# A mask added in the tiling of the attention scores, and the scores computed in two sets

## The chip, the cores and the metric

The kernel runs on one core of a Trainium2 chip. The metric is the device time of one execution in microseconds (us). TensorE multiplies matrices into PSUM banks, VectorE and ScalarE read PSUM and work on rows, GpSimd (POOL) works on SBUF and issues indirect transfers, SyncE issues most of the other transfers.

## The reference, cut to what matters

Two transformer layers over 64 sequences of 64 tokens of width 128. Each has a layer norm, a cross attention to a context of 64 tokens per sequence with 16 heads of width 8, and a mixture of experts (one of 8 experts in layer 0, two of 16 in layer 1). Only the attention of layer 0 has a mask:

```
x = x + tanh(g_xattn[0]) * attention0(layernorm(x), ctx, ctx, mask)   # 16 heads
    scores = where(mask == 0, -1e9, q @ k.T);  softmax(scores / sqrt(8)) @ v
x = x + tanh(g_ffn[0]) * top1_of_8_experts(layernorm(x))
x = x + tanh(g_xattn[1]) * attention1(layernorm(x), ctx, ctx)         # no mask
x = x + tanh(g_ffn[1]) * top2_of_16_experts(layernorm(x))
```

## The kernel before

The 4096 tokens are 32 tiles of 128 rows, two sequences each. Tiles are taken in ten groups of 2, 2, 4, 4, 4, 4, 4, 4, 2, 2 (SIZES), for layer 0 and again for layer 1, so tiles count from 0 to 63; a unit is a pair of tiles. The stages of the trace are: attention of layer 0 (with its router) to about 170 us, experts of layer 0 to about 275 us, attention of layer 1 to about 425 us, then the experts of layer 1.

The order of the work on each engine is written out by hand. A step has a list of items (tiles, units or groups) and a function that gives each item a place in time, counted in tiles; run() sorts all steps of an engine by that place and, within one place, by their order in the list. `shift(-2)` for tile t is place t - 2, `head(-4)` for a group is its first tile - 4, `tail(3)` its last tile + 3. Each engine works off its list in order; waits on semaphores (`wait_ge`) keep the engines together.

For one tile t the attention goes like this:

- GpSimd builds k_blk (L427): the keys of four heads side by side with zeros elsewhere, in a ring of two.
- TensorE computes scores (L852): for each of two sequences b and four row groups q of 32 rows (four heads each) one f32 product of 32 x 64 weights and 256 columns, at the position (32 q, 64 b) of the array. Row groups 0 and 1 go into S_ps[0], 2 and 3 into S_ps[1], each two PSUM banks. It waits for qT, for k_blk, and for `shifted` to show that both halves of tile t - 1 were read.
- In layer 0 the mask goes into the banks ahead of the scores (L829): an identity of 128 x 128 in bf16 times mask_bias (0 or -2^100), a bank at a time, over four heads. mask_first does S_ps[0], at the place t - 2 behind the transposes of the tile before, as soon as its first half was subtracted; score does S_ps[1] and then all products, at the place t - 1.
- VectorE takes for each half h the maximum over keys (L593) and subtracts it (L601), which frees that half of the banks: maximum(0), subtract(0), maximum(1), subtract(1), at the place t - 1. Both halves wait for the one semaphore `scored`.
- TensorE transposes each half (L863; half 0 at the place t - 1, half 1 at the place t), ScalarE takes exp (L530), TensorE multiplies with the values (L878), VectorE divides (L609, L612).

Around this, per group or unit, run the projections of q, k and v (L825, L737, L748), the output (L895) and its addition on VectorE (L620), and the router's turns, logits and ranks. TensorE's list within one place is: score, turn_probs(1), ranks, attend, logits, turn_av, project_q, output, project_v, project_k, turn_probs(0), mask_first, turn_r, turn_x.

The raw mask is loaded by SyncE per group (L401) as 128 rows x 64 columns of int32 per tile, eleven tiles ahead, in a ring of four, and cast by VectorE per group four tiles ahead (L648). SyncE's list holds x, ctxT, the mask, and the rows kept for the second layer (L406).

Of the kernel before, what the change touches and what calls it, by code (L numbers as in the profile page):

```python
# [6 lines left out]
BF16 = mybir.dt.bfloat16  # L7
# [7 lines left out]
H, DK = 16, 8  # L15
# [108 lines left out]
def head(skew):  # L124
    return lambda g: g.first + skew


def tail(skew):
    return lambda g: g.last + skew
# [55 lines left out]
def attention(nc, ctx, space, x_all, r_xn, ws, dram, rs, hooks):  # L185
# [67 lines left out]
    ctx_loaded = [sem(f"ctx_loaded{k}") for k in range(CR)]  # L253
    mask_loaded = [sem(f"mask_loaded{k}") for k in range(R)]
    kept = [sem("kept_full"), sem("kept_rest")]
# [16 lines left out]
    kblk_ready = sem("kblk_ready")  # L272
    scored = sem("scored")
    max_ready = sem("max_ready")
    shifted = sem("shifted")
# [38 lines left out]
    def of(layer):  # L314
# [26 lines left out]
        def dram_rows(g):  # L341
            return slice(g.local * P, (g.local + g.n) * P)
# [41 lines left out]
        def sync_steps(sp):  # L384
            def load_x(g):
                if g.i >= 4:
                    sp.wait_ge(ln_stats, units_to(g.i - 4))
                from_ = dram["x"] if masked else r["x_mid"]
                sp.dma_start(x_group(g), from_[dram_rows(g), :].rearrange("(u p) d -> p u d", p=P)).then_inc(x_in[g.at(4)], 16)

            def load_ctx(g):
                if g.i >= CR:
                    sp.wait_ge(k_made, g.i - CR + 1)
                    sp.wait_ge(v_made, units_to(g.i - CR))
                sp.dma_start(ctxT[:, g.at(CR), 0:g.n, :],
                             dram["ctxT"][:, dram_rows(g)].rearrange("d (u p) -> d u p", p=P)).then_inc(ctx_loaded[g.at(CR)], 16)

            def load_mask(g):
                if g.i >= R:
                    sp.wait_ge(mask_made, g.i - R + 1)  # L400
                sp.dma_start(mask_in[:, g.at(R), 0:g.n, :],  # L401
                             dram["mask"][dram_rows(g), :].rearrange("(u p) k -> p u k", p=P)).then_inc(mask_loaded[g.at(R)], 16)
# [186 lines left out]
        def vector(dve):  # L589
            def maximum(h):  # L590
                def step(t):
                    dve.wait_ge(scored, t + 1)
                    nc.vector.tensor_reduce(maxes[:, t % 2, h, :, :], half_of(h), X, ALU.max).then_inc(max_ready, 1)  # L593
                return step
# [48 lines left out]

            def mask(g):
                n, at = g.n, g.at(R)
                dve.wait_ge(mask_loaded[at], 16 * (g.i // R + 1))
                wait(dve, scored, tiles_to(g.i - R))
                nc.vector.tensor_scalar(mask_bias[:, at, 0:n, :], mask_in[:, at, 0:n, :], 0.0, MASKED, ALU.is_equal, ALU.mult).then_inc(mask_made, 1)  # L648

# [71 lines left out]
            if masked:  # L721
                steps += [(choose, groups, settled(6, 11, short, later)), (rows, groups, settled(7, 12, short, later)), (mask, groups, head(-4))]
# [44 lines left out]
        def tensor(pe):  # L767
# [58 lines left out]

            def mask_half(h, g, u):
                for k in range(2):
                    nc.tensor.matmul(S_ps[h][:, k, 0:HQ * S].rearrange("p (e k) -> p e k", k=S), w["ident_bf"][:, :],  # L829
                                     mask_bias[:, g.at(R), u, :].unsqueeze(1).to_broadcast([P, HQ, S]),  # L830
                                     start=True, stop=False, skip_group_check=True)

            def mask_first(t):
                g = GROUP_OF[t]
                pe.wait_ge(mask_made, g.i + 1)
                if t == 0:
                    pe.wait_ge(r["casts"], 1)
                wait(pe, shifted, 2 * t - 1)
                mask_half(0, g, t - g.first)

            def score(t):
                g = GROUP_OF[t]
                u = t - g.first
                pe.wait_ge(qT_ready, g.i + 1)
                pe.wait_ge(kblk_ready, t + 1)
                wait(pe, shifted, 2 * t)
                if masked:
                    mask_half(1, g, u)
                for b in range(2):
                    for q in range(4):  # L850
# [4 lines left out]
                last.then_inc(scored, 1)  # L855

# [43 lines left out]
            awake += [] if masked else [(lambda n: stream_into(T_ps, n), [Q], lambda _: NT - 1)]  # L900
            steps = [score_ahead] + awake + [(turn_probs(1), tiles, shift(0)),
                     (rank if masked else rank_slots, groups, settled(7 if masked else 8, 12, short, later)), (attend, tiles, shift(1)), (logit, groups[:7], settled(6, 9, short, later)),
                     (turn_av, groups, tail(2)), (project_q, groups, head(-2)), (output, groups, tail(3)),
                     (logit, groups[7:], settled(6, 9, short, later)),
                     (project_v, late_units, unit_head(-1)), (project_k, late, head(-3)),
                     (turn_probs(0), tiles, shift(-1)), (mask_first, tiles if masked else [], shift(-2)), (turn_r, groups, settled(5, 8, short, later)), (turn_x, groups, turn_x_at)]
            run(hook["first_tensor"](pe) + steps + hook["tensor"](pe))
# [628 lines left out]

IN_A = [("ident", P), ("wq", D), ("wk", D), ("bq", 1), ("bk", 1), ("bv", 1), ("head_rows", H // 4), ("tile_at", 1), ("row_at", 1)]
IN_B = [("wv", D), ("wo", D), ("before0", P), ("before1", P), ("ones1", P), ("router0", E0), ("router1", E1)]
# [33 lines left out]
def program(nc, d, out):  # L1572
    with ExitStack() as ctx:
# [18 lines left out]
        w1.update(cut(col_1, IN_1))  # L1592
        w0.update(bo=w0["bo0"], minus_half=sb("minus_half", [P, Q]), eps=sb("eps", [P, Q]), ident_bf=sb("ident_bf", [P, P], BF16))
        w1.update(bo=w0["bo1"])
# [16 lines left out]
        r1.update(before=bf["before1_bf"], ones=bf["ones1_bf"], router=w0["router1"])  # L1611
        r0["pads"] = Space(nc, space.at).take("pads", [P, PADS, RW])
        f1 = r1["f1"] = {"in": sem("f1_weights_in")}
        for name, shape in (("gate", [P, E1, HID1]), ("fc", [P, E1, HID1]), ("proj", [P, E1 // 2, D])):
            f1[name] = sb("f1_" + name, shape)
        for name, shape, dt in (("logits", [P, NT, E1], F32), ("top", [P, NT, 8], F32), ("top_at", [P, NT, 8], U32), ("slot", [P, 2, NT], F32),
                                ("sent", [P, 2, NT], F32), ("gap", [P, NT], F32), ("total", [P, NT], F32)):
            r1[name] = sb("r1_" + name, shape, dt)

        late = Space(nc, space.at)  # L1620
# [41 lines left out]
        def lay_bv(_):  # L1662
            vec = nc.vector
            vec.wait_ge(in_a, 16)
            vec.tensor_copy(bv_rows[:, 0, :], w0["bv"].to_broadcast([P, P])).then_inc(bv_laid, 1)
            vec.tensor_copy(w0["ident_bf"][:, :], w0["ident"][:, :]).then_inc(r0["casts"], 1)
            vec.wait_ge(in_1, 16)
            vec.tensor_copy(bv_rows[:, 1, :], w1["bv"].to_broadcast([P, P])).then_inc(bv_laid, 1)
# [207 lines left out]
```

## Time and profile before

| | |
|---|---|
| time before, median of 3 runs | 513.66 us (513.63 to 516.26) |
| the profiled execution | 512.48 us, its span 510.7 us |
| granted TensorE clock, mean | 0.983 |
| busy share of the span | PE 86 %, DVE 70 %, ACT 63 %, POOL 53 % |
| chain that ended last, by engine | PE 43 %, DVE 23 %, issue 18 %, POOL 7 % |
| data moved in the first 12.8 us | 209 GB/s |

A busy PE is not PE at its peak, since the ends of matmuls are modelled. PE is TensorE, DVE VectorE, ACT ScalarE. A line such as L852 is that of the kernel before.

### The profile page before, as it was taken

The numbers are of one execution on the slowest core, as the hardware profiler recorded it, in microseconds if no ns is written. First come the engines' busy times: TensorE is split into PE (matmuls) and PEld (weight loads), VectorE is DVE, ScalarE is ACT, GpSimd is POOL, SyncE is SP. The second block draws the span as 40 slices with busy tenths as digits, with TensorE's granted clock in tenths as the row PEclk, the third lists the DMA queues.
The fourth block names the chain that finished last, engine by engine and source line by source line (L and its number), as shares of the span: only waits on it lengthen the run. The fifth ranks groups of instructions, "written<-read, shape, count | busy, mean of one in ns | idle before, by whom it ended". The sixth has DMA issues, their size and how long they took to land.

```text
span 510.7 us, 21982 instructions
## 1 busy us (share of the span) xinstructions
PE 438.4 (86%) x8481; PEld 321.1 (63%) x8481; DVE 359.5 (70%) x949; ACT 322.7 (63%) x755; POOL 272.7 (53%) x325
## 2 busy tenths in 40 slices
PE   2788999799978785999998789998999688798986
PEld 1455677567756685999983456666667456554544
DVE  5778879878778765455541788889998787664555
ACT  2555575566766783677754556776778467676663
POOL 2632535545475268888886544544552481544444
PEclk9999999999999998899999899999999899999999
DMA  7225434232110145565436001110031000000112
GB/s 209 51 57 153 98 104 126 70 106 71 46 55 29 35 126 101 78 97 71 45 35 148 14 4 45 46 33 3 25 85 35 23 4 4 3 1 16 43 42 68
DMA packets 50629, 30.69 MB, mean 60 GB/s; under 512 B 12384, under 2 KB 46944, under 8 KB 50528
## 3 DMA queue, kind: packets, MB, share of 16 engines
q1 hardware_dynamic: 37072, 18.54, 13.6%
q0 software_dynamic: 6640, 4.67, 7.0%
q10 hardware_dynamic: 6816, 6.07, 4.2%
q8 instruction: 70, 1.15, 0.9%
q14 instruction: 31, 0.25, 0.2%
HBM read 19.41 MB, written 9.85 MB: 57 GB/s over the span
## 4 chain that ended last, share of the span: by engine, by line
PE 43%; DVE 23%; issue 18%; POOL 7%; ACT 4%; DMA 3%; ACTq 1%; DVEq 1%; POOLq 0%; SPq 0%
DVE maxes L593 8%; PE S_ps L852 6%; PE T_ps L863 5%; POOL x_mid L1145 4%; PE A_ps L878 4%; PE m_H_ps L1478 3%; DVE prob L601 3%; PE S_ps L829 2%; PE m_X_ps L1505 2%; PE Q_ps L825 2%; PE m_T_ps L1518 2%; PE f_H_ps L1197 2%; PE Q_ps L737 2%; PE m_X_ps L1489 2%; PE m_X_ps L1461 2%
## 5 line engine op out<-in xcount | busy, mean ns | idle before, releaser
L593 DVE TENSOR_REDUCE maxes<-S_ps 128x8 f32<-128x512 f32 x128 | 87.6, 685 | 40.5 <-PE S_ps L852 40.5
L427 POOL TENSOR_TENSOR k_blk<-kT,col_a 128x512 f32<-128x512 f32 x64 | 67.7, 1068 | 77.7 <-ACT kT L488 54.5
L530 ACT ACTIVATE probT<-T_ps 128x512 f32<-128x512 f32 x128 | 76.0, 594 | 43.5 <-PE T_ps L863 42.8
L863 PE MATMUL T_ps<-col_a,prob 128*128 128x128 f32 x512 | 83.4, 287 | 9.8 <-DVE prob L601 6.1
L601 DVE TENSOR_TENSOR prob<-S_ps,maxes 128x512 f32<-128x512 f32 x128 | 88.5, 692 | 4.4
L863 PEld LDWEIGHTS T_ps<-col_a,prob 128*128 128x128 f32 x512 | 56.7, 143 | 48.0 <-issue 34.4
L1145 POOL DMA_INDIRECT x_mid<-f_out,f_rows x39 | 60.9, 1562 | 11.9 <-issue 11.9
L852 PE MATMUL S_ps<-k_blk,qT 32*64 32x256 f32 x1024 | 46.5, 415 | 5.0 <-DVE prob L601 4.1
L1010 DVE TENSOR_TENSOR f_hid<-f_H_ps,f_b 128x512 f32<-128x512 f32 x39 | 27.0, 692 | 32.4 <-PE f_Y_ps L1211 27.0
L878 PE MATMUL A_ps<-v_blk,probT 128*32 128x18 f32 x4096 | 48.7, 187 | 0.2 <-issue 0.2
L878 PEld LDWEIGHTS A_ps<-v_blk,probT 128*32 128x32 f32 x4096 | 42.0, 110 | 9.7 <-issue 8.8
L1197 PE MATMUL f_H_ps<-f_rowsT,f_w_now 128*128 128x128 f32 x312 | 42.5, 280 | 4.7 <-ACT f_rowsT L1156 4.7
L1211 PE MATMUL f_Y_ps<-f_w,f_hid 128*128 x312 | 42.6, 281 | 0.7 <-ACT f_hid L1168 0.6
L1197 PEld LDWEIGHTS f_H_ps<-f_rowsT,f_w_now 128*128 128x128 f32 x312 | 39.1, 197 | 4.9 <-ACT f_rowsT L1156 4.9
L464 POOL DMA_INDIRECT sorted_rows<-r_xn,row x32 | 32.1, 1003 | 14.4 <-DVE row L673 7.0
L1211 PEld LDWEIGHTS f_Y_ps<-f_w,f_hid 128*128 128x128 f32 x312 | 38.8, 195 | 1.3 <-issue 1.1
L513 ACT ACTIVATE xn<-x_all,shift_by,rstd 128x128 f32<-128x128 f32 x64 | 31.0, 493 | 10.7 <-DVE shift_by L631 10.7
L497 ACT COPY v_blk<-Q_ps 64x256 f32<-64x256 f32 x64 | 23.9, 373 | 19.4 <-PE Q_ps L748 18.9
L1387 POOL TENSOR_SCALAR m_other<-row_constants,r_slot,r_gap 128x128 f32<-128x128 f32 x32 | 25.4, 800 | 19.7 <-DVE m_combine L1354 19.3
L449 POOL TENSOR_TENSOR x_all<-x_all,row_constants 128x512 f32<-128x512 f32 (+1 forms) x20 | 21.1, 1056 | 25.3 <-ACT xn L513 20.9
L1168 ACT ACTIVATE f_hid<-f_hid 128x512 f32<-128x512 f32 x39 | 24.6, 631 | 15.8 <-DVE f_hid L1010 15.7
L456 POOL TENSOR_SCALAR r_spread<-r_stats 128x4 f32<-128x4 f32 (+1 forms) x20 | 3.9, 194 | 55.5 <-DVE r_stats L642 55.5
(200 smaller groups left out, 867.6 us busy)
## 6 DMA issues: line engine op xcount, KB each, us to landing
f_w<-in_W ACTq DMA_DIRECT2D x16, 256.0 KB, 2.8
ctxT<-in_ctxT SPq DMA_DIRECT2D x12, 256.0 KB, 3.0
f_rows<-sorted_rows SPq DMA_DIRECT2D x39, 64.5 KB, 2.0
out<-m_final SPq DMA_DIRECT2D x32, 64.0 KB, 1.5
x_all<-in_x SPq DMA_DIRECT2D x6, 256.0 KB, 5.8
x_mid<-x_all SPq DMA_DIRECT2D x6, 256.0 KB, 2.5
x_all<-x_mid SPq DMA_DIRECT2D x6, 256.0 KB, 3.6
ctxT<-in_ctxT SPq DMA_DIRECT2D x8, 128.0 KB, 2.6
```

Source lines behind the costliest of these rows:

```text
L427: nc.gpsimd.tensor_tensor(k_blk[:, t % 2, :, :, :], kT[:, g.at(R), t - g.first, :].rearrange("p (b k) -> p b k", b=2).unsqueeze(2).to_broa ...
L464: pool.indirect_dma_start(r["sorted"], bass.IndirectOffsetOnAxis(ap=row[:, t:t + 1], axis=0), r_xn[:, t, :], None).then_inc(scattered[t >= ...
L513: nc.scalar.activation(xn[:, g.at(XR), u, :], x_of(t), ACT.Identity, bias=shift_by[:, g.i % NR, u:u + 1], scale=rstd[:, g.i % NR, u:u + 1] ...
L530: nc.scalar.activation(probT[:, t % 2, 4 * h:4 * h + 4, :], T_ps[:, :, :], ACT.Exp, scale=SCALE).then_inc(probT_ready, 1)
L593: nc.vector.tensor_reduce(maxes[:, t % 2, h, :, :], half_of(h), X, ALU.max).then_inc(max_ready, 1)
L601: nc.vector.tensor_tensor(prob[:, t % 2, heads, :].rearrange("p (r e) k -> p r e k", r=2), half_of(h), maxes[:, t % 2, h, :, :].unsqueeze( ...
L852: last = nc.tensor.matmul(S_ps[q // 2][b * S:(b + 1) * S, q % 2, 0:HQ * S], qT[rows, g.at(R), u, b * S:(b + 1) * S], k_blk[rows, t % 2, b, ...
L863: last = nc.tensor.transpose(T_ps[:, j, :], pair, ident[:, :])
L878: last = nc.tensor.matmul(AV[queries, m + j, :], probT[:, t % 2, j, queries], v_blk[:, g.at(R), t - g.first, c * part // S, j, :], start=T ...
L1145: pool.indirect_dma_start(r["x_mid"], bass.IndirectOffsetOnAxis(ap=rows[:, t % RINGS, D:RW].bitcast(I32), axis=0), out[:, t % DEEP, :], No ...
L1197: last = pe.matmul(H_ps[t % 2][:, n, :], w1_now[:, t % 2, n * P:(n + 1) * P], rowsT[:, t % 2, :], start=True, stop=True)
L1211: last = pe.matmul(Y_ps[t % 2][:, 0:D], hid[:, t % 2, n, :], w2[:, bass.ds(e, 1), n, :].rearrange("p a c -> p (a c)"), start=n == 0, stop= ...
```

## The change

The mask comes from the host four times as wide: row 32 q + i of a tile holds, for each of the four 32-row strips of the tile's queries, the mask row i of that strip (4 x 64 columns), and the same again for each row group q. So each row group holds the whole mask of the tile. A constant shift32 (128 x 128, cast to bf16 in place of the identity) puts 32 such rows at the first or second half of 64 output rows. The mask is added by matmuls of 32 x 64 weights, two for each position (32 q, 64 b), one for each strip: 16 per tile instead of 4. The raw mask has a ring of two groups, in memory shared with the second layer's weights, and is asked for seven tiles ahead (the first two groups eleven); it is cast per unit.

The scores of both layers are now two steps. score_first does mask and products of row groups 0 and 1 and signals `scored_first`, on which maximum(0) waits; it needs only the first half of tile t - 1 to be subtracted and stands at the end of the place t - 2, behind turn_r and turn_x (the first two tiles of a layer: right ahead of score). score does row groups 2 and 3. mask_half and mask_first are gone.

```
-    mask_in = sb("mask_in", [P, R, Q, S], I32)
-    mask_bias = sb("mask_bias", [P, R, Q, S], BF16)
+    MR = 2
+    mask_in = rs[0]["mask_in"]
+    mask_bias = sb("mask_bias", [P, MR, Q, 4 * S], BF16)
...
-                if g.i >= R:
-                    sp.wait_ge(mask_made, g.i - R + 1)
-                sp.dma_start(mask_in[:, g.at(R), 0:g.n, :],
+                wait(sp, mask_made, units_to(g.i - MR))
+                sp.dma_start(mask_in[:, g.at(MR), 0:g.n, :],
...
-                steps += [(load_mask, groups, head(-11)), (keep, groups, tail(5))]
+                steps += [(load_mask, groups, lambda g: g.first - (11 if g.i < MR else 7)), (keep, groups, tail(5))]
...
-                    dve.wait_ge(scored, t + 1)
+                    if h == 0:
+                        dve.wait_ge(scored_first, t + 1)
+                    else:
+                        dve.wait_ge(scored, t + 1)
...
-                nc.vector.tensor_scalar(mask_bias[:, at, 0:n, :], mask_in[:, at, 0:n, :], 0.0, MASKED, ALU.is_equal, ALU.mult).then_inc(mask_made, 1)
+                nc.vector.tensor_scalar(mask_bias[:, at, k, :], mask_in[:, at, k, :], 0.0, MASKED, ALU.is_equal, ALU.mult).then_inc(mask_made, 1)
...
-(mask, groups, head(-4))
+(mask, units, lambda u: u.first - 4)
...
+            def mask_set(t, quarters):
...
+                for part in range(2):
+                    for b in range(2):
+                        for q in quarters:
+                            rows = slice(q * 32, (q + 1) * 32)
+                            at = 2 * b + part
+                            nc.tensor.matmul(S_ps[q // 2][b * S:(b + 1) * S, q % 2, 0:HQ * S].rearrange("p (e k) -> p e k", k=S),
+                                             w["shift32_bf"][rows, part * S:(part + 1) * S],
+                                             mask_bias[rows, g.at(MR), t - g.first, at * S:(at + 1) * S].unsqueeze(1).to_broadcast([32, HQ, S]),
+                                             start=part == 0, stop=False, skip_group_check=True, tile_position=(q * 32, b * S))
...
+            def score_first(t):
+                pe.wait_ge(qT_ready, GROUP_OF[t].i + 1)
+                pe.wait_ge(kblk_ready, t + 1)
+                wait(pe, shifted, 2 * t - 1)
+                if masked:
+                    mask_set(t, (0, 1))
+                products(t, (0, 1)).then_inc(scored_first, 1)
+
+            def score(t):
+                wait(pe, shifted, 2 * t)
+                if masked:
+                    mask_set(t, (2, 3))
+                products(t, (2, 3)).then_inc(scored, 1)
...
-                     (turn_probs(0), tiles, shift(-1)), (mask_first, tiles if masked else [], shift(-2)), (turn_r, groups, settled(5, 8, short, later)), (turn_x, groups, turn_x_at)]
+                     (turn_probs(0), tiles, shift(-1)), (turn_r, groups, settled(5, 8, short, later)), (turn_x, groups, turn_x_at), (score_first, split[2:], shift(-2))]
```

## Rows read from the trace of the kernel before

**Rows 1.** Windows: us, PE, PEld, DVE, ACT, POOL busy, PEclk, DMA share, GB/s.
```profile
22.00:168.00 146.00, 131.31 (x3288) 93.00 (x3280) 118.82 (x270) 91.10 (x197) 73.32 (x84) 0.99 0.30 82
288.00:423.00 135.00, 117.92 (x3136) 83.56 (x3135) 115.91 (x288) 90.35 (x224) 63.77 (x90) 0.98 0.11 29
```

**Rows 2.** Waits of VectorE, 18 to 170 us: total us, times, longest.
```profile
DVE maxes L593 <- PE S_ps L852: 23.7, 20, 3.2
```

**Rows 3.** Waits of VectorE, 284 to 425 us.
```profile
DVE maxes L593 <- PE S_ps L852: 16.8, 21, 3.0
```

**Rows 4.** Waits of TensorE, 18 to 170 us.
```profile
PE S_ps L829 <- DVE prob L601: 2.3, 5, 0.5
PE X_ps L798 <- issue: 1.9, 1, 1.9
PE T_ps L863 <- DVE prob L601: 1.6, 3, 0.6
...
PE S_ps L829 <- POOL k_blk L427: 0.7, 1, 0.7
```

**Rows 5.** Waits of TensorE, 284 to 425 us.
```profile
PE T_ps L863 <- DVE prob L601: 4.5, 4, 2.5
PE S_ps L852 <- DVE prob L601: 4.1, 8, 0.8
PE T_ps L863 <- ACT probT L530: 2.3, 11, 0.3
```

**Rows 6.** Timeline of a tile of layer 0: start, us, engine, line [idle before].
```profile
75.00 0.69 DVE L601 TENSOR_TENSOR prob<-S_ps,maxes 128x512 f32<-128x512 f32 x1
...
75.14 0.38 PE L829 MATMUL S_ps<-mask_bias,ident_bf 128*128 128x256 bf16 x2
...
75.36 0.38 PE L788 MATMUL X_ps<-col_a,r_xn 128*128 128x128 f32 x2
...
75.83 0.38 PE L829 MATMUL S_ps<-mask_bias,ident_bf 128*128 128x256 bf16 x2
...
76.14 0.69 PE L852 MATMUL S_ps<-k_blk,qT 32*64 32x256 f32 x16
...
76.76 0.66 PE L863 MATMUL T_ps<-col_a,prob 128*128 128x128 f32 x4
...
76.94 0.69 DVE L593 TENSOR_REDUCE maxes<-S_ps 128x8 f32<-128x512 f32 x1 [0.91 <-PE S_ps L852]
```

**Rows 7.** Timeline of a tile of layer 1.
```profile
333.75 0.69 DVE L601 TENSOR_TENSOR prob<-S_ps,maxes 128x512 f32<-128x512 f32 x1
...
335.37 0.69 DVE L593 TENSOR_REDUCE maxes<-S_ps 128x8 f32<-128x512 f32 x1 [0.59 <-PE S_ps L852]
```

**Rows 8.** Timeline of VectorE: four of the first maxima that waited.
```profile
26.20 0.69 DVE L593 TENSOR_REDUCE maxes<-S_ps 128x8 f32<-128x512 f32 x1 [0.72 <-PE S_ps L852]
...
118.31 0.69 DVE L593 TENSOR_REDUCE maxes<-S_ps 128x8 f32<-128x512 f32 x1 [0.29 <-PE S_ps L852]
...
287.97 0.69 DVE L593 TENSOR_REDUCE maxes<-S_ps 128x8 f32<-128x512 f32 x1 [1.40 <-PE S_ps L852]
...
399.16 0.69 DVE L593 TENSOR_REDUCE maxes<-S_ps 128x8 f32<-128x512 f32 x1 [0.17 <-PE S_ps L852]
```

**Rows 9.** The score matmuls' line: ns min/median/max, first and last start.
```profile
L852 PE MATMUL S_ps<-k_blk,qT x1024: 374/425/685, 16.8 to 422.1; 32*64 32x256 f32 x171
```

**Rows 10.** The mask cast's line, the same columns.
```profile
L648 DVE TENSOR_SCALAR mask_bias<-mask_in x10: 217/280/744, 14.7 to 150.6; 128x256 bf16<-128x256 int32 x6, 128x128 bf16<-128x128 int32 x4
```

**Rows 11.** Transfers issued from 0 to 60 us: count, size, median us to landing.
```profile
f_b<-in_b ACTq DMA_DIRECT2D x1, 512.0 KB, 3.7
sorted_rows<-pads SPq DMA_DIRECT2D x1, 451.5 KB, 5.5
```

**Rows 12.** Chain of waits, 0 to 24 us: start, us, what.
```profile
2.22 6.89 DMA col<-in_col
...
14.77 0.44 DVE mask_bias L648
```

More of the change, by code:

```diff
@@ L253, in attention @@
     ctx_loaded = [sem(f"ctx_loaded{k}") for k in range(CR)]
-    mask_loaded = [sem(f"mask_loaded{k}") for k in range(R)]
+    mask_loaded = [sem(f"mask_loaded{k}") for k in range(MR)]
     kept = [sem("kept_full"), sem("kept_rest")]
@@ L273, in attention @@
     scored = sem("scored")
+    scored_first = sem("scored_first")
     max_ready = sem("max_ready")
@@ L642, in r_stat, with mask @@
                 nc.vector.bn_stats(pair_of(r_stats[:, g.i % 2, :, :], u), x_pair(u)).then_inc(r_stats_ready, 1)
[L644 to L647, printed above, removed]
-                nc.vector.tensor_scalar(mask_bias[:, at, 0:n, :], mask_in[:, at, 0:n, :], 0.0, MASKED, ALU.is_equal, ALU.mult).then_inc(mask_made, 1)
+            def mask(u):
+                g, k = u.group, slice(2 * u.k, 2 * u.k + u.n)
+                at = g.at(MR)
+                dve.wait_ge(mask_loaded[at], 16 * (g.i // MR + 1))
+                wait(dve, scored, tiles_to(g.i - MR))
+                nc.vector.tensor_scalar(mask_bias[:, at, k, :], mask_in[:, at, k, :], 0.0, MASKED, ALU.is_equal, ALU.mult).then_inc(mask_made, 1)
             def choose(g):
@@ L721, in vector @@
             if masked:
-                steps += [(choose, groups, settled(6, 11, short, later)), (rows, groups, settled(7, 12, short, later)), (mask, groups, head(-4))]
+                steps += [(choose, groups, settled(6, 11, short, later)), (rows, groups, settled(7, 12, short, later)), (mask, units, lambda u: u.first - 4)]
             else:
@@ L825, in project_q, with products @@
                 nc.tensor.matmul(Q_ps[:, 0:g.n, :], w["wq"][:, :], xnT[:, 0:g.n, :], start=True, stop=True).then_inc(q_made, 1)
[L827 to L833, printed above, removed]
+            def mask_set(t, quarters):
                 g = GROUP_OF[t]
-                pe.wait_ge(mask_made, g.i + 1)
+                pe.wait_ge(mask_made, g.units[(t - g.first) // 2].i + 1)
                 if t == 0:
                     pe.wait_ge(r["casts"], 1)
-                wait(pe, shifted, 2 * t - 1)
-                mask_half(0, g, t - g.first)
-            def score(t):
+                for part in range(2):
[7 more added lines that the diff above has]
+                                             start=part == 0, stop=False, skip_group_check=True, tile_position=(q * 32, b * S))
+            def products(t, quarters):
                 g = GROUP_OF[t]
                 u = t - g.first
[L844 to L848, printed above, removed]
                 for b in range(2):
-                    for q in range(4):
+                    for q in quarters:
                         rows = slice(q * 32, (q + 1) * 32)
@@ L900, in tensor @@
             awake += [] if masked else [(lambda n: stream_into(T_ps, n), [Q], lambda _: NT - 1)]
-            steps = [score_ahead] + awake + [(turn_probs(1), tiles, shift(0)),
+            split = tiles
+            steps = [(score_first, split[:2], score_at), score_ahead] + awake + [(turn_probs(1), tiles, shift(0)),
                      (rank if masked else rank_slots, groups, settled(7 if masked else 8, 12, short, later)), (attend, tiles, shift(1)), (logit, groups[:7], settled(6, 9, short, later)),
@@ L1611, in program @@
         r1.update(before=bf["before1_bf"], ones=bf["ones1_bf"], router=w0["router1"])
-        r0["pads"] = Space(nc, space.at).take("pads", [P, PADS, RW])
+        first_only = Space(nc, space.at)
+        r0["pads"] = first_only.take("pads", [P, PADS, RW])
+        r0["mask_in"] = first_only.take("mask_in", [P, 2, Q, 4 * S], I32)
         f1 = r1["f1"] = {"in": sem("f1_weights_in")}
@@ L1665, in lay_bv @@
             vec.tensor_copy(bv_rows[:, 0, :], w0["bv"].to_broadcast([P, P])).then_inc(bv_laid, 1)
-            vec.tensor_copy(w0["ident_bf"][:, :], w0["ident"][:, :]).then_inc(r0["casts"], 1)
+            vec.tensor_copy(w0["shift32_bf"][:, :], w0["shift32"][:, :]).then_inc(r0["casts"], 1)
             vec.wait_ge(in_1, 16)
@@ L1830 @@
     arrays = {
-        "x": i["x"].reshape(T, D), "ctxT": i["ctx_1024"].reshape(T, D).T, "mask": i["mask_BxSxS2_ik1"].reshape(T, S),
+        "x": i["x"].reshape(T, D), "ctxT": i["ctx_1024"].reshape(T, D).T, "mask": np.tile(i["mask_BxSxS2_ik1"].reshape(NT, 4, 32, S).transpose(0, 2, 1, 3).reshape(NT, 1, 32, 4 * S), (1, 4, 1, 1)).reshape(T, 4 * S),
     }
@@ L1847 @@
     columns["head_rows"] = (p[:, None] // DK % (H // 4) == np.arange(H // 4)[None, :]).astype(np.float32)
+    columns["shift32"] = (np.arange(P)[None, :] // S * 32 + p[:, None] % 32 == np.arange(P)[None, :] % S).astype(np.float32)
     columns["tile_at"] = p.astype(np.float32)
```

9 lines of the change are left out of this document (5 added, 4 removed).

## The prediction

> **What bounds the kernel now.** I read the windows of the two attention layers first, then who waits for whom on VectorE and on TensorE there, then the timeline of two tiles. In 146 us of layer 0 TensorE is busy for 131.3 us and VectorE for 118.8; in 135 us of layer 1 it is 117.9 and 115.9 [rows 1]. So neither is full, TensorE lacks 14.7 and 17.1 us, and the reader is to see that the time goes in turns: now the one waits, now the other. VectorE waits for the scores (the first maximum of a tile, L593, for L852) 20 times in layer 0 for 23.7 us and 21 times in layer 1 for 16.8 us [rows 2, 3]. TensorE waits for the subtraction (L601) before masks, transposes and scores for 3.9 and 8.6 us [rows 4, 5].
>
> The timeline shows why both can be idle. In layer 0 the last subtraction of a tile ends at 75.69; only then may the second half of the mask start (75.83), the scores follow at 76.14, and the maximum at 76.94, 1.25 us after the subtraction [rows 6]. In layer 1, without a mask, the same loop takes 0.93 us (334.44 to 335.37) [rows 7]. A tile in which TensorE stood ready for that subtraction can be told by this fixed distance. There are 7 such waits of VectorE in layer 0, the first of 0.72 us and the last of 0.29, together 4.95 us, and 12 in layer 1, the first of 1.40 and the last of 0.17, together 7.16 us [rows 8]. These 12.1 us are the wait that the change goes at. The other 28.4 of 40.5 us are tiles in which TensorE itself came late, with projections, router work or a stall in front.
>
> **The change, part by part.**
>
> *Scores in two sets.* The first set (row groups 0 and 1, into the first pair of banks) needs only the first subtraction of the tile before, which ends 1.3 us ahead of the second one (two VectorE operations of 0.69) [rows 6]. It stands behind that tile's first transposes, which wait for the same subtraction, so it adds no wait of its own on the shift. It does add waits on qT and k_blk at this point, with the whole of TensorE's queue behind them; but the scores that stood next in the queue had them already, and k_blk, made one or two tiles ahead, was late once in all [rows 4]. So the first maximum of the next tile finds its scores ready when the second subtraction ends, and the second maximum comes 1.4 us later, when the second set (ready some 0.8 us after that subtraction) is done too. Up to 12.1 us go. Not all: where the sets don't run back to back, each pays its own fill and its own change of tiling, some 0.3 us more of TensorE per tile, and TensorE's own waits for the subtraction before masks and scores are 0.46 and 0.51 us in the mean [rows 4, 5], so in some tiles it becomes the one that is late. I take three quarters, -9 us; the ends are -3 and -12.1.
>
> *Where the sets stand side by side.* With TensorE late, the first set is the last thing in one turn of its loop and the second set the first in the next, with nothing between. What the pair costs then isn't in the trace, so from both sides. Before: 0.22 us for two masks (75.14 to 75.36), 0.31 for the other two with the change to small tiles, 0.62 for the scores, 1.15 us in all [rows 6]. After, a set with its mask has two mask passes one behind the other in each tile of the array (0.11 each) and the products, about 0.82 us. If the second set runs beside the first, on the two row groups that this leaves free, the pair takes about 0.9; if it starts only when the first has issued its last product, about 1.5. So between -0.25 and +0.35 us per tile in layer 0, and between 0 and +0.27 in layer 1. The row nearest to it: the 16 matmuls of a tile's scores last 0.37 to 0.43 us each [rows 9] and all of them are through in 0.62 us [rows 6], so small tiles do run beside one another. I take -0.1 us on some 20 late tiles of layer 0, -2 us, and nothing in layer 1; the ends are -5 and +9.
>
> The Trainium skill ("TensorE: Matmul & The Clock Gate", Part 3, "What overlaps and what doesn't") says that matmuls start and end in program order, whatever row group they use. By it the second set waits for the first one's last product, the dearer end above; no row of this trace separates the two, as the merged timeline shows only that all 16 overlap. By that rule the sum below would be about 9 us higher.
>
> *Four-fold mask on VectorE.* Ten casts become sixteen of 128x512. The six of 128x256 take 0.280 us (the median), the quickest of 128x128 0.217 [rows 10], so 0.063 us per 128 columns: 0.41 us for 512 by that slope, 0.56 if twice the larger. That is 6.5 to 9 us against some 3.4 now (six at 0.28, the other four between 0.22 and 0.74), 3 to 5.6 us more. VectorE has 27 idle us in layer 0 [rows 1], and with the score wait gone less of them; I let 1.5 us come through, ends 0 and 5.
>
> *Four-fold mask in the queues.* A group's mask is now 512 KB. Transfers of 451.5 and 512 KB landed after 5.5 and 3.7 us [rows 11]. SyncE asks for it three tiles ahead of its cast, some 14 us, at the place in its queue where a mask stood before, between the context and the x of other groups; its wait on mask_made is for a cast three tiles back. So it is covered; were each of the eight later groups 1 us late, it would cost 8 us, and that is in the range only through the rival below.
>
> *The start.* Up to 9 us the transfers are the chain: the fourth weight block is on its way from 2.22 to 9.11 [rows 12]. Ahead of or beside it now lie 64 KB more of constants (shift32) and 2 x 192 KB more mask, less 128 KB that moves behind; at the 209 GB/s of the page's first slice the 320 KB take 1.5 us, part of it off the chain. The first cast, 0.44 us in the chain [rows 12], gets 0.2 us longer, and the third mask now lands near 25 us, about when it is cast. I take +1.5 us, ends +0.5 and +3.
>
> *What changes nothing.* A separate 32-row shift matrix in place of the identity, the two new rings of the mask, and the shared memory for the raw mask add no instruction on a full engine. TensorE's 384 further mask matmuls are in the set's price.
>
> **Sum.** -9 - 2 + 1.5 + 1.5 = -8.0 us. The profiled execution took 512.48 us (span 510.7), so 504.5; the median shown is 1.2 us above it, so about 505.5 us.
>
> **Rivals.**
>
> 1. *The two loops come apart altogether (17 in 100).* VectorE's maximum no longer follows TensorE's latest scores, and a heavy turn of one engine is spread over two turns of the other. For it: 31.8 idle us on TensorE with VectorE at 81 to 86 % [rows 1]. Against: part of it is router chains and single stalls of 1.9 and 2.5 us [rows 4, 5]. Two thirds of it back, -21, less the 3 us of start and casts: -18, 495.5 us.
>
> 2. *The wait only moves (17 in 100).* TensorE's transposes wait for exp (11 times in layer 1 [rows 5]) and for the router's steps; in a turn in which turn_x or turn_r, now ahead of the first set, waits for a group's output to be added, the first set is no earlier than the scores were. Then a quarter of the 12.1 us is left, -3, and start and casts eat it: 512.5 to 514, no change.
>
> 3. *The sets follow one another (9 in 100), slower.* Place: TensorE between two tiles. Price: +0.35 us in layer 0 and +0.27 in layer 1 on 17 late tiles (41 waits less the 19 ready ones and some five behind a stall), 5.3 us; the ready tiles keep half their gain, -4.5; start and casts +3. Sum +3.8, 517.5 us. It decides from the point where the pair costs more than about 1.4 us in layer 0.
>
> 4. The forecast, 57 in 100.
>
> **Range and chances.** Within 0.5 % (2.6 us) is about what a measurement of this kernel can't tell from no change. Faster: nearly all of the forecast's case (0.55) and rival 1, 0.72. Same: rival 2 and the forecast's upper edge, 0.18. Slower: rival 3 and a late mask, 0.10. The range goes from a little below rival 1's time to rival 2's upper end, 493 to 514.5 us.
>
> **What would show it.** Right: in both layers the maximum of the first half no longer stands 1.25 or 0.93 us behind the subtraction, VectorE's wait for scores falls from 40.5 to under 28 us, the span of layer 0's and layer 1's 30 inner tiles falls by some 4 us each, and the first maximum (18.05 us on the profile's axis) comes 1 to 2 us later. The pair of sets in a late tile of layer 0 takes 1.0 to 1.1 us. Wrong: a gap between the first set's last matmul and the second set's first although the subtraction is done; VectorE waiting for the second maximum instead; a wait of TensorE or VectorE on a mask's transfer behind the start; or both layers as long as before with the score wait gone.

## The result, and the profile after

The changed kernel took 519.99 us (median of 4, 519.16 to 521.48) against 513.64: 1.0132 times as long, 95 % interval 1.0088 to 1.0177. The prediction of 505.5 us (493 to 514.5) was wrong, and by its sign. Run again on another chip it took 519.44 us (12 runs) against 514.58, ratio 1.0028 (0.9988 to 1.0068). Ratios leave out executions more than 1.5 % above the fastest of their kernel, here 5 of the 12 (at a granted clock of 0.943 to 0.960) and 2 of the 23 of the kernel before, so they can differ from the ratio of two medians. The two measurements differ mostly by TensorE's clock: over the 177 executions that the ratios of this study keep, a line through time and mean granted clock, one level for each kernel, gives 2.1 +- 0.2 us for each 0.01 of clock, and the first four stood at 0.957 to 0.973, the kernel before at 0.981 in the mean. By this line, at equal clock, the changed kernel is 2.1 +- 0.6 us slower. "At equal clock" below always means this line; it takes the clock as given, though a kernel may bring its own.

The profile after has a span of 517.6 us, 6.9 more. By the starts of the first maxima these lie so (us; layer 0 from tile 1 to 31, layer 1 from tile 32 to 63, tail from there to the end):

| kernel | tile 0 | tile 0 to 1 | layer 0 | 31 to 32 | layer 1 | tail |
|---|---|---|---|---|---|---|
| before | 18.05 | 4.16 | 146.02 | 115.62 | 138.78 | 88.06 |
| after | 19.00 | 5.24 | 147.57 | 115.93 | 135.93 | 93.96 |
| after, second profile | 19.28 | 5.24 | 152.41 | 115.68 | 135.75 | 90.63 |

Layer 1 gained 3 us, layer 0 lost 1.5 to 6.4, the tail, whose instructions are the same, 2.6 to 5.9.

Windows of the profile after, columns as in [rows 1]: layer 0, then a stretch of layer 1.

```profile
24.24:171.81 147.57, 133.86 (x3648) 96.27 (x3644) 121.80 (x279) 90.56 (x197) 74.34 (x83) 0.99 0.35 98
293.00:428.00 135.00, 124.02 (x3252) 87.73 (x3250) 119.61 (x294) 92.09 (x229) 62.59 (x89) 0.98 0.11 29
```

Both engines are a little busier than in [rows 1] in both layers, and DMA's share in layer 0 went from 0.30 to 0.35.

VectorE's waits after, 20 to 174 us and then 288 to 430 us (total, times, longest):

```profile
DVE maxes L597 <- PE S_ps L853: 20.7, 18, 3.7
DVE x_all L624 <- PE X_ps L910: 2.7, 3, 1.1
...
DVE maxes L597 <- PE S_ps L853: 11.3, 15, 1.9
DVE x_all L624 <- PE X_ps L910: 0.9, 1, 0.9
```

The wait for scores fell from 40.5 us [rows 2, 3] to 32.0, near the 9 us forecast, though not under the 28 that the prediction named as its sign. Most of the fall is in layer 1. In layer 0 it is 3.0 us, and a wait that was not there before stands beside it: 2.7 us at the residual add (L624) for TensorE's output (L910). VectorE started earlier and then stood at the next thing that TensorE had not done.

TensorE's waits after, 20 to 174 us, then 288 to 430 us:

```profile
PE S_ps L853 <- issue: 1.6, 2, 0.8
PE Q_ps L753 <- issue: 1.4, 2, 1.1
PE X_ps L803 <- issue: 1.3, 1, 1.3
PE S_ps L842 <- issue: 0.8, 2, 0.6
...
PE T_ps L878 <- DVE prob L605: 4.4, 4, 2.7
PE T_ps L878 <- ACT probT L531: 2.3, 11, 0.3
```

TensorE's waits for the subtraction before masks and scores, 2.3 us in layer 0 [rows 4] and 4.1 in layer 1 [rows 5], are gone (the second profile has one left, of 1.5 us in layer 0). In their place layer 0 has waits for nothing that the profile shows (`issue`): 5.6 us between 25 and 172 us, 9.0 in the second profile, 1.9 before [rows 4].

Last, the tail: a window of 24 us of before, then of after.

```profile
429.00:453.00 24.00, 18.91 (x282) 12.89 (x284) 15.69 (x77) 18.52 (x58) 12.47 (x26) 1.00 0.01 2
```

```profile
429.00:453.00 24.00, 21.10 (x224) 14.80 (x224) 12.30 (x62) 14.58 (x46) 9.38 (x20) 0.57 0.01 2
```

The mean clock was 0.57: for 20.5 us TensorE ran at 1.2 GHz instead of 2.4, and did 224 matmuls where it had done 282.

### The profile page after: what moved, and what is told of

Same layout as the page of the kernel before. It is cut to its first block, busy times and chain, and to the rows that moved or that the text cites. A ratio compares the mean times of both kernels' runs of the same rounds, so it can differ in the third digit from the quotient of the medians.

```text
span 517.6 us, 22796 instructions
## 1 busy us (share of the span) xinstructions
PE 454.2 (88%) x8865; PEld 333.6 (64%) x8865; DVE 364.2 (70%) x955; ACT 322.9 (62%) x755; POOL 273.8 (53%) x325
## 4 chain that ended last, share of the span: by engine, by line
PE 57%; DVE 16%; issue 12%; POOL 5%; ACT 4%; DMA 4%; ACTq 1%; DVEq 1%; SPq 0%; POOLq 0%
PE T_ps L878 9%; PE S_ps L853 6%; PE A_ps L893 5%; DVE maxes L597 5%; PE f_H_ps L1213 4%; PE f_Y_ps L1227 4%; PE m_H_ps L1494 3%; PE Q_ps L830 3%; PE m_X_ps L1477 3%; PE S_ps L842 3%; POOL x_mid L1161 3%; PE Q_ps L753 2%; PE X_ps L910 2%; PE Q_ps L742 2%; PE m_X_ps L1521 2%
## 5 line engine op out<-in xcount | busy, mean ns | idle before, releaser
L878 PE MATMUL T_ps<-col_a,prob 128*128 128x128 f32 x512 | 85.0, 290 | 9.9 <-DVE prob L605 6.3
L853 PE MATMUL S_ps<-k_blk,qT 32*64 32x256 f32 x1024 | 56.9, 405 | 2.5 <-issue 1.6
L893 PE MATMUL A_ps<-v_blk,probT 128*32 128x18 f32 x4096 | 50.4, 188 | 0.8 <-issue 0.7
L893 PEld LDWEIGHTS A_ps<-v_blk,probT 128*32 128x32 f32 x4096 | 43.1, 112 | 10.8 <-issue 9.5
L498 ACT COPY v_blk<-Q_ps 64x256 f32<-64x256 f32 x64 | 23.9, 373 | 20.5 <-PE Q_ps L753 20.1
L450 POOL TENSOR_TENSOR x_all<-x_all,row_constants 128x512 f32<-128x512 f32 (+1 forms) x20 | 21.1, 1055 | 25.6 <-ACT xn L514 23.8
```

The source lines that it names most:

```text
L878: last = nc.tensor.transpose(T_ps[:, j, :], pair, ident[:, :])
L893: last = nc.tensor.matmul(AV[queries, m + j, :], probT[:, t % 2, j, queries], v_blk[:, g.at(R), t - g.first, c * part // S, j, :], start=T ...
```

## The experiments

**One part alone.** `split_only`: two sets in both layers, masks in 128x128 and loads as before. `mask_only`: the new masks, one set of scores, the first half's mask at its old place. `split_l1`: layer 0 as before, layer 1 as changed. `after_again`: the changed kernel.

```diff
 # split_l1
-steps = [score_ahead] + awake + [...(mask_first, tiles if masked else [], shift(-2)), ...]
+steps = [(score_first, [] if masked else tiles[:2], score_at), score_ahead] + awake + [...(mask_first, ...), ...,
+         (score_first, [] if masked else tiles[2:], shift(-2))]
```

> The scores of both layers in two sets as in the change, but mask loads, casts and the 128x128 mask matmuls as before. Theory 'clock' (the attention has gained some 4 us, and the rest of the loss is TensorE standing longer at 1.2 GHz in other stages): attention of layer 1 from the first maximum of tile 35 to that of tile 63 takes 124 to 125 us as after the change (before 127.3), layer 0 from tile 1 to 28 takes 129 to 132 us (before 131.4), and the total goes with the clock: 508 to 511 us at a mean clock of 0.98, 515 to 518 at 0.96. Rival 'mask work' (the four-fold mask costs the time): 505 to 509 us whatever the clock. Rival 'split' (the split itself costs): 518 us or more, and layer 1 no shorter than before.

> The four-fold mask and its 32x64 matmuls as in the change, but the scores of a tile in one set at their old place, the first half of the mask put down where it stood before. Theory 'clock': layer 0 from tile 1 to 28 as before within 2 us, layer 1 as before (127.3 us from tile 35 to 63), start 1 us later, total 514 to 516 us at a clock of 0.98 and some 5 us more at 0.96. Rival 'mask work': 518 to 522 us, with layer 0 longer by 5 us or more between tile 1 and 28. Rival 'split': 511 to 515 us.

> Only layer 1's scores in two sets, layer 0 wholly as before. Theory 'clock': layer 0 and the start as before, layer 1 from tile 35 to 63 in 124 to 125 us (before 127.3), total 510 to 511 us at a clock of 0.98, more by half of the time at 1.2 GHz beyond the 17 us of before. Rival 'split': 515 us or more with layer 1 no shorter. Rival 'mask work': 508 to 511 us whatever the clock.

> The changed kernel once more, for a second profile of it. Theory 'clock': 515 to 522 us; the stages in which TensorE stands at 1.2 GHz are others than in the first profile (there 432 to 453 us after layer 1's attention, 159 to 163 us in layer 0, and the start up to 26 us), and the stage times without them agree with the first profile within 1 us. Rivals 'mask work' and 'split': 519 to 522 us with the same stages long, whatever the clock.

Measured: `split_only` 521.42 us, ratio to before 1.0160 (1.0109 to 1.0211); `mask_only` 525.43, 1.0197 (1.0141 to 1.0253); `split_l1` 512.07, 0.9954 (0.9916 to 0.9993). So layer 1's split is a gain, of some 2 us, and in layer 0 each of the two parts alone is a loss, larger than both together. That takes the clock as the only cause away. No theory fits all of it: `mask_only` lies above the highest range named for it, and `split_only` lies where 'split' put it, but with layer 1 shorter (124.6 us from tile 35 to 63), which 'split' had ruled out. The two profiles of the changed kernel differ by 4.8 us in layer 0, where 'clock' allowed 1.

Why the split costs in layer 0 is seen in TensorE's timeline: one tile's masks and scores before, then with the split alone.

```profile
84.66 0.70 PE L829 MATMUL S_ps<-mask_bias,ident_bf 128*128 128x256 bf16 x4
85.28 0.69 PE L852 MATMUL S_ps<-k_blk,qT 32*64 32x256 f32 x16
85.90 0.66 PE L863 MATMUL T_ps<-col_a,prob 128*128 128x128 f32 x4
```

```profile
73.29 0.38 PE L830 MATMUL S_ps<-mask_bias,ident_bf 128*128 128x256 bf16 x2
73.60 0.66 PE L840 MATMUL S_ps<-k_blk,qT 32*64 32x256 f32 x8
74.20 0.39 PE L830 MATMUL S_ps<-mask_bias,ident_bf 128*128 128x256 bf16 x2
74.52 0.66 PE L840 MATMUL S_ps<-k_blk,qT 32*64 32x256 f32 x8
75.11 0.66 PE L871 MATMUL T_ps<-col_a,prob 128*128 128x128 f32 x4
```

The eight f32 products of a tile stand in the trace as sixteen matmuls (1024 for 64 tiles [rows 9]). These sixteen take 0.69 us; eight alone, on two of four row groups, take 0.66. With a 128x128 mask between them the sets do not run beside one another: 1.82 us where it was 1.24. In the changed kernel the masks have the scores' tiling, and the pair does run side by side:

```profile
77.68 0.44 PE L842 MATMUL S_ps<-mask_bias,shift_bf 32*64 32x256 bf16 x12
77.92 0.39 PE L853 MATMUL S_ps<-k_blk,qT 32*64 32x256 f32 x4
77.95 0.28 PE L842 MATMUL S_ps<-mask_bias,shift_bf 32*64 32x256 bf16 x4
78.06 0.60 PE L853 MATMUL S_ps<-k_blk,qT 32*64 32x256 f32 x12
78.59 0.65 PE L878 MATMUL T_ps<-col_a,prob 128*128 128x128 f32 x2
```

0.91 us for all of it. Twelve masks start before the first product, so four masks of the second set start ahead of the first set's products, which stand before them in the list. So the new masks are what makes the split bearable. Why the masks without the split cost most of all was not taken apart: the one profile of `mask_only`, of its slowest execution, has 10.1 us of unexplained waits of TensorE between 25 and 172 us.

The trace shows more: the second set follows the first at once. By the starts of matmuls 8 and 9 of each tile, the sets are over 0.35 us apart in 3 of 30 inner tiles of layer 0 (in the median 0.08 us) and in 4 of 30 of layer 1. The first set stands an iteration's end ahead in the order, but TensorE comes to it so late that the second may start too. It is not ahead in time.

**What bounds layer 0.** `add_last` puts VectorE's add behind the choices and casts of its iteration (in layer 1 to the same end of the list), `narrow_cast` casts 32 of 512 columns, `no_mask` leaves the mask matmuls out, `together` puts the first set directly before the second.

```diff
 # add_last
-(divide, units, unit_end(1)), (add, groups, tail(3)), ... (mask, units, ...)]
+(divide, units, unit_end(1)), ... (mask, units, ...), (add, groups, tail(3))]
 # together
-steps = [(score_first, split[:2], score_at), score_ahead] + ... (score_first, split[2:], shift(-2))]
+steps = [(score_first, tiles, score_at), score_ahead] + ...]
 # no_mask
-if masked:
-    mask_set(t, ...)
```

> The changed kernel, with VectorE's residual add put behind the chain of choices, the group rows and the mask casts of the same iteration, so that TensorE's output has longer to arrive. In the changed kernel VectorE stands 8.2 us over both layers (7 waits in the page's row) for the output matmuls at the add, 2.7 to 4.5 of it in layer 0, which the kernel before did not. 'Array' (TensorE is what bounds layer 0: a set of half the heads uses two of its four row groups, so masks and scores of a tile take it 1.56 us where they took 1.41): the add's wait goes, but the first maxima then wait that much longer: 517.5 to 521 us, no change from 519.5. Rival 'queue' (VectorE's added serial work and this wait eat the gain): the wait is gained, 514.5 to 517.

> The changed kernel without the mask matmuls on TensorE (the masks are loaded and cast as before but not added, so the scores are unmasked). They take TensorE 19.3 us for 30 tiles of layer 0. 'Array': TensorE bounds layer 0, so most of them is gained: the stretch from tile 1 to tile 31 goes from 148 to 152 us down to 132 to 139, the whole to 503 to 510 us. Rival 'queue': VectorE's chain bounds it, the masks lie beside it, and 3 to 6 us are gained, 513.5 to 517.

> The changed kernel with the first set no longer an iteration's end ahead but directly in front of the second, both where the scores stood before. 'Array': the sets run side by side and masks and scores of a tile take TensorE 1.3 to 1.4 us again, with the first maximum waiting as before; layer 0 within 2 us of the kernel before plus the casts (146 to 150 us from tile 1 to 31), layer 1 back to 103 to 104 us from tile 35 to 59: 514 to 519 us. If instead the masks' tiling and the casts are what costs ('mask work'), the time stays at 519 to 526 us, as with the four-fold masks alone (525.4).

> The changed kernel with only 32 of each 512 mask columns cast on VectorE (the rest of the biases is zero, so most masks are left out; loads and TensorE's mask matmuls stay). 5.8 us of casts in layer 0 become some 1.3. 'Queue': VectorE's chain is the bound and 3.5 to 4.5 us come back, 515 to 516.5 us. 'Array': TensorE is the bound, VectorE waits for the scores instead, 517.5 to 520.5 us.

Measured: `add_last` 520.98 us, 1.0129 (1.0079 to 1.0180); `no_mask` 507.17, 0.9843 (0.9784 to 0.9903); `together` 517.19, 1.0030 (0.9991 to 1.0068); `narrow_cast` 518.78, 1.0102 (1.0050 to 1.0154). VectorE's waits in `add_last`, 25 to 172 us:

```profile
DVE maxes L597 <- PE S_ps L853: 24.6, 22, 3.8
DVE x_all L624 <- PE X_ps L910: 1.0, 1, 1.0
```

The wait at the add went and the wait for scores grew, as 'array' expected. With the casts cut (from 7.5 to 3.9 us of VectorE) the time did not move by a measurable amount either. TensorE's work did move it: without the mask matmuls a tile's masks and scores go from 1.13 to 0.75 us of TensorE (start to next start, standstills left out), 11 us in layer 0, and 9.6 +- 1.0 us of the whole came back at equal clock. The total, 507 us, lies in what was expected; layer 0 took 144.3 us in the profile, not 132 to 139, with two stretches at 1.2 GHz in it. So layer 0's time follows TensorE's work, and VectorE's waits there are slack. It does not follow one to one: in `split_only` a tile's masks and scores cost TensorE 0.6 us more, some 18 us in layer 0, and the stretch from tile 1 to 31 grew by 5.3, since TensorE's idle time in it fell from 14.7 to 4.5 us. `no_mask` also has fewer instructions to fetch, which the next part comes to. `together` equals the changed kernel: having the first set ahead in the order is worth nothing that can be measured.

The price in 'array', 1.56 us a tile for 1.41, is wrong: it adds two lines' busy times, and after the change masks and products overlap. From start to next start, standstills left out, it is 1.22 us before and 1.12 to 1.14 after. TensorE's work for masks and scores fell, so what costs in layer 0 is something else.

**The width of the mask loads.** In TensorE's unexplained waits there is one that stops in the middle of a set of scores (after, layer 0):

```profile
86.99 0.50 PE L842 MATMUL S_ps<-mask_bias,shift_bf 32*64 32x256 bf16 x13
87.23 0.39 PE L853 MATMUL S_ps<-k_blk,qT 32*64 32x256 f32 x4
...
87.33 0.59 PE L853 MATMUL S_ps<-k_blk,qT 32*64 32x256 f32 x7
...
88.72 0.65 PE L853 MATMUL S_ps<-k_blk,qT 32*64 32x256 f32 x5 [0.80 <-issue]
```

Eleven of the sixteen matmuls have started and the last five come 0.80 us later, with no operand to wait for. What may have been missing are instructions. The page lists a queue named instruction, q8, with 70 packets and 1.15 MB before, 73 and 1.20 MB after: 16 KB each, and TensorE's 17,948 recorded instructions before, weight loads and semaphores among them, are 256 for each of the 70. Transfers from 82.9 to 86.4 us, and from 86.4 to 86.5 (packets, MB, share of 16 engines):

```profile
q1 hardware_dynamic: 1117, 0.85, 77.5%
q10 hardware_dynamic: 89, 0.17, 12.9%
...
q8 instruction: 1, 0.02, 54.8%
```

One such fetch began at 86.45, 2.3 us before TensorE went on. By the count of instructions since the earliest fetch of layer 0 it was due near 82.9. In between q1 kept the DMA engines busy for 77.5 % of the time. What SyncE had asked for shortly before, from its timeline:

```profile
81.00 0.34 SPq L397 DMA_DIRECT2D ctxT<-in_ctxT  x1
81.39 0.45 SPq L407 DMA_DIRECT2D x_mid<-x_all  x1
81.88 0.51 SPq L402 DMA_DIRECT2D mask_in<-in_mask  x1
82.44 0.67 SPq L391 DMA_DIRECT2D x_all<-in_x  x1
```

Four transfers in 1.5 us, and the mask of 512 KB is the largest; it was 128 KB before. The Trainium skill ("Runtime: NRT & Kernel Launch", "Instruction fetch mechanics") says that such blocks come over a DMA queue of the sequencer's own and that this is mostly hidden. By this timing it is not hidden here where other transfers fill the engines. Waits of TensorE of over 0.25 us that end 1.8 to 3 us after the start of a late fetch (one that begins 130 or more instructions behind the earliest of layer 0) sum up in layer 0 to 1.9 us before, 2.6 and 6.3 in the two profiles after, 8.8 in `add_last` and 0 in `split_only`. Over all fifteen profiles of this study the sum is 0 to 2.6 us in the six kernels with narrow mask loads and 2.6 to 9.5 in the nine profiles with wide ones; it moves by up to 2.5 us with where late begins.

To try it, `small_loads` loads 64 of 256 mask columns and spreads them in the same cast (three of four blocks carry another's mask), `wide_loads` is the kernel before with each mask row stored four times over and loaded whole, at the changed kernel's times and with its two buffers, and `spread_loads` cuts the changed kernel's loads in two.

```diff
 # small_loads
-sp.dma_start(mask_in[:, g.at(MR), 0:g.n, :], dram["mask"][dram_rows(g), :]...)
+sp.dma_start(mask_in[:, g.at(MR), 0:g.n, 0:S], dram["mask"][dram_rows(g), 0:S]...)
 # wide_loads
-"mask": i["mask_BxSxS2_ik1"].reshape(T, S),
+"mask": np.tile(i["mask_BxSxS2_ik1"].reshape(T, S), (1, 4)),
 # spread_loads
-(load_mask, groups, lambda g: g.first - (11 if g.i < MR else 7))
+(load_mask, units, lambda u: u.first - (11 if u.group.i < MR else 7))
```

> The changed kernel with only 64 of the 256 mask columns of a row loaded (the cast spreads them over all four blocks, so three of four blocks carry the mask of another; TensorE and VectorE do the same instructions). 'Fetch' (the 512 KB loads of masks hold up the 16 KB fetches of TensorE's instructions, which then stands without work: 5.6 to 9.0 us of unexplained idle time in layer 0 against 1.9): that idle time falls to 1 to 4 us, and 2 to 5 us come back: 514 to 517.5 us. Rival 'instructions' (TensorE simply has more matmuls and signals): 518.5 to 521.

> The kernel before with only its mask loads made four times as wide (each mask row is stored four times over and loaded whole, one copy is cast as before) and put at the changed kernel's times with two buffers. 'Fetch': TensorE's unexplained idle time in layer 0 goes from 1.9 to 4 to 9 us and the time by 2 to 5 us above the kernel before: 516.5 to 519.5. 'Instructions': the kernel before to within 1 us: 513.5 to 515.5.

> The changed kernel with each mask load cut in two by pairs of tiles, the second two tiles later; bytes, casts and TensorE's work stay. If it is the burst that holds up other transfers (the fetches of TensorE's instructions among them), most of what the narrow loads gave comes back: 514 to 517 us. If the bytes as such cost, it stays with the changed kernel: 518 to 520.5.

Measured: `small_loads` 513.64 us, 0.9989 (0.9960 to 1.0018); `wide_loads` 515.85, 1.0042 (1.0009 to 1.0076); `spread_loads` 516.98, 1.0016 (0.9982 to 1.0050). Layer 0 of `small_loads`, from tile 1 to 31 (146.02 before, 147.57 and 152.41 after):

```profile
24.14:169.43 145.29, 131.11 (x3648) 95.18 (x3644) 122.92 (x279) 90.61 (x197) 73.84 (x83) 1.00 0.30 82
```

The same instructions with a quarter of the mask's bytes: 3.6 +- 0.8 us less than the changed kernel at equal clock, inside the 2 to 5 us that 'fetch' expected to come back. The two ratios alone, 0.9989 and 1.0028, have intervals that overlap. In the kernel before, the wide loads cost 1.9 +- 0.6 us at equal clock, and 515.85 lies between the two expectations (its unexplained waits are 3.6 us, where 'fetch' expected 4 to 9). So the width of the loads is a cost, and in the changed kernel it is as large as the whole loss at equal clock, 2.1. The path is shown less well. The unexplained waits were expected to fall to 1 to 4 us and stand at 6.8, between the two profiles after. The waits behind late fetches are 2.6 us, as in the first of these and under half of the second. In `wide_loads` they grew from 1.9 to 2.8. Over the seven profiles with the same TensorE work in layer 0 the unexplained waits and the time go together, which shows no cause yet: the three with 5.6 to 6.8 us of unexplained waits took 145 to 149 us from tile 1 to 31, the four with 9.0 to 12.6 us took 151.6 to 152.4. `spread_loads` decides nothing: 516.98 is in the range of the burst, but the kernel before took 516.70 on that chip, its interval overlaps that of `after_again`, and at equal clock the two are the same (-0.4 +- 0.8).

**What layer 1 gained from, and the sum of the gains.** `signal_only` is the kernel before with the products at their place, the first maximum's heads first, and a signal behind the first half. `best` has that in layer 0 and the changed kernel's order in layer 1.

```diff
 # signal_only
-for b in range(2):
-    for q in range(4):
-        ...
-last.then_inc(scored, 1)
+for quarters, done_sem in (((0, 1), scored_first), ((2, 3), scored)):
+    for b in range(2):
+        for q in quarters:
+            ...
+    last.then_inc(done_sem, 1)
```

> The kernel before, masks and loads as they were, with one difference in both layers: the sixteen products stand in the same place in two sets, heads of the first maximum first, and the first set signals by itself. Nothing runs ahead. 'Signal' (the set ahead in the order is not ahead in time, because TensorE reaches both sets late; what layer 1 gained is only that the first maximum starts when half the products are done): layer 1's stretch from tile 35 to 59 shortens by 1.5 to 2.5 us as in the changed kernel, layer 0 by 0 to 5 us, since a set lies 0.22 us behind the other: 506 to 511.5 us against 514.7 for the kernel before. Rival 'ahead' (the place an iteration's end ahead is what gains): 513 to 515.5.

> Layer 0 with the masks, loads and place of the kernel before, its products in two sets side by side with a signal behind the first; layer 1 as in the changed kernel, the first set an iteration's end ahead. If the gains are separate, they add up: 3.1 us in layer 0 (the stretch from tile 1 to 31 at 143 us) and 2.0 in layer 1 (tile 35 to 59 at 101.5 to 102 us), so 507 to 510 us beside 514.5 for the kernel before. If TensorE in layer 0 only shifts what it is late with, as in the changed kernel, it stays at 511 to 513.

Measured: `signal_only` 512.88 us, 0.9947 (0.9912 to 0.9982); `best` 508.55, 0.9876 (0.9824 to 0.9929), the fastest kernel here that adds the masks, 6.4 us below before by the ratio. TensorE's waits in layer 1 (284 to 425 us), `signal_only`, then `best`:

```profile
PE S_ps L854 <- DVE prob L602: 5.4, 11, 0.8
PE T_ps L865 <- DVE prob L602: 4.5, 4, 2.5
```

```profile
PE T_ps L879 <- DVE prob L605: 4.4, 4, 2.5
PE T_ps L879 <- ACT probT L531: 2.6, 12, 0.3
```

'Signal' was wrong on layer 1: with the signal alone the stretch from tile 35 to 59 stays at 103.59 us (103.85 before, 101.97 after). What gains there is that the first set no longer waits for the second subtraction, so TensorE's wait before scores is gone in `best`. It is not the place in the list: `together`, whose first set stands where the scores stood but waits for the first subtraction alone, took 102.07. The early signal is worth less than the 0.22 us that I gave it: in the 20 waiting tiles of layer 0 the first maximum starts 0.73 us after the first product instead of 0.79 (medians). The trace's starts show why: the two sets interleave, and the last matmul of the first set, which gives the signal, starts 0.03 us before the last of all (median). Layer 0 took 142.95 us in `signal_only` but 145.98 in `best`, with the same instructions there; the first lacked a stall near 98 us and a stretch of low clock behind it that `best` and before have. So those 3 us of layer 0 are not shown to be the signal's, though the ratio of `signal_only`, with its whole interval below 1, says that something was gained. `best` keeps layer 1's gain. What else makes it faster than `split_l1` (1.8 +- 0.9 us at equal clock) was not taken apart.

## Why the prediction was wrong

*Scores in two sets, -9 (ends -3 and -12.1): failed.* The wait was counted on VectorE, 12.1 us. VectorE's wait for scores did fall by 8.5 us, but layer 0's time follows TensorE, and VectorE's wait came back at the add or, with that moved, at the scores. What could be gained was TensorE's own wait for that subtraction, 2.3 us in [rows 4] and 4.1 in [rows 5]. It did go, but for 1.5 us in one of two profiles. In layer 1 this gave 2 us from tile 35 to 59 and 3 over the whole layer; in layer 0 nothing that can be told from the rest. Rival 2, the wait that only moves, was right for layer 0, by another route: not turn_x or turn_r, but the output and TensorE as a whole.

*The pair side by side, -2 (ends -5 and +9): right in layer 0.* 1.22 us a tile became 1.12 to 1.14, 2.4 to 3 us over 30 tiles, and the pair takes 0.91 us, near the cheap end. Rival 3, sets that follow one another, did not come. The rule of program order that the prediction cites from the Trainium skill ("TensorE: Matmul & The Clock Gate", Part 3, "What overlaps and what doesn't") is not borne out here: at 77.68 twelve masks start before the first product, where the list has eight. (By its own ends, -2 and +9, that rule would have put the sum 11 us higher, not 9.) In layer 1 I took nothing and it cost 0.14 us a tile (0.65 to 0.79), some 4 us over its tiles. TensorE's idle time there fell by more than the 4.1 us of that wait, from 18.9 to 12.3 us, and about 3 us were left.

*Casts, +1.5 (ends 0 and 5): the lower end.* They take 0.42 us each (the median), as the slope said, and are covered.

*Mask transfers, covered: failed, and this turned the sign.* I asked whether a mask lands in time for its cast, and it does. I did not ask what its bytes hold up. Their width costs 3.6 +- 0.8 us at equal clock; without it the changed kernel is at 0.9989 (0.9960 to 1.0018) of the kernel before.

*Start, +1.5: about right.* The first maximum came 0.95 us later, inside the ends. The further 1.1 us to tile 1 are in nearly all profiles, `split_l1` among them, whose start is that of before; there the clock first stood at 2.4 GHz at 23.8 us, in the profile of before at 19.2.

Together, as an estimate from these rows: -2 to -3 us in layer 1, +3.6 for the width of the loads and +1 to +2 at the start make some +1.5 to +3.5 us, and 2.1 was measured at equal clock.

*Not in the sum: the clock.* Some 3 us of the first measurement. A long stretch at 1.2 GHz (14 to 24 us, beginning between 427 and 442 us) was in five of the nine profiles of the changed kernel and the variants made from it (after, `add_last`, `small_loads`, `mask_only`, `no_mask`), and in none of the six of the kernel before and its variants. Whether the change brings it is open: no run took it apart.

## What to carry to other kernels

Where two engines wait for each other in turns, price the removal of a wait on the engine that is busier: its own idle time at that wait, here 2.3 and 4.1 us, came nearer to what came back than the other's 12.1. Standing earlier in a queue is not running earlier; look in the timeline for whether the engine reaches that place before its release. A transfer that lands in time for its reader can still cost, so look at what else is moving then, the fetches of instructions among it.

## What the runs showed of the hardware

Eight score matmuls on two row groups take 0.66 us and sixteen on four 0.69: a set of half the row groups alone occupies TensorE nearly as long as a whole one, while two such sets back to back, with masks of the same tiling, take 0.91 us in all. The trace has them interleaved, not one behind the other. TensorE's instructions come in fetches of 16 KB for 256 instructions, some 5 us apart in layer 0. One that began 3.6 us late by the count of instructions, after a stretch in which the kernel's own transfers on q1 kept the DMA engines busy for 77.5 %, was followed 2.3 us later by the end of a standstill of TensorE of 0.80 us in the middle of a set. That the transfers held the fetch up is argued from this timing and from the sums over fifteen profiles; no run moved the fetches alone.
